# Whole rows normalised and stored beside the eighth expert's products, its slots' rows normalised singly and written over

## What is computed

```
x = x + xattn(layernorm(x), ctx)
h = layernorm(x)                                  # [4096, 256]
gates, idx = top_k(softmax(h @ wg), 2)            # renormalised
# every expert takes at most C = 1280 of its tokens
y = silu(disp @ fc1_w.T + fc1_b) @ fc2_w + fc2_b  # for each expert, 256 -> 1024 -> 256
res = h + sum over the two experts of gate * y
out = x + (res - mean(res)) * rsqrt(var(res) + 1e-5) * gamma + beta
```

## Time and profile before

| | |
|---|---|
| median of 3 runs | 764.63 us (762.34 to 767.64) |
| the profiled execution | 763.03 us, its span 761.3 us |
| busy PE / DVE / ACT / POOL | 672.8 / 551.4 / 409.8 / 419.7 us |
| mean granted clock of TensorE, share of full speed | 0.94 |
| DMA | 64.81 MB, mean 85 GB/s |

### The profile page before, as it was taken

The page is one execution under the profiler, slowest core; times in us unless marked ns, Lnnn a source line. Parts: engine busy times, 40 slices in busy tenths (PEclk is TensorE's granted clock), DMA queues, the critical chain, the costliest instruction groups (busy, mean ns, idle before and its releaser), DMA issues.

```text
span 761.3 us, 15549 instructions
## 1 busy us (share of the span) xinstructions
PE 672.8 (88%) x5562; PEld 643.6 (85%) x5562; DVE 551.4 (72%) x1129; ACT 409.8 (54%) x956; POOL 419.7 (55%) x541
## 2 busy tenths in 40 slices
PE   4999999999999645999999999999999999999500
PEld 3799999999988534999999998999999999999500
DVE  6578888888888795766566689687696566855187
ACT  6355555555555583545445475555555455634185
POOL 5445665665663426254544668576585653631456
PEclk9699999999999956999999999999999999999855
DMA  9710111111101124244334346453555342322474
GB/s 295 208 37 31 43 37 35 43 35 37 43 30 43 42 76 140 72 98 100 55 93 106 57 106 123 110 111 59 113 114 113 74 78 47 59 33 24 71 261 152
DMA packets 61348, 64.81 MB, mean 85 GB/s; under 512 B 15057, under 2 KB 56529, under 8 KB 61137
## 3 DMA queue, kind: packets, MB, share of 16 engines
q1 hardware_dynamic: 45201, 42.35, 17.7%
q0 software_dynamic: 15360, 21.31, 17.3%
q10 hardware_dynamic: 704, 0.01, 0.0%
HBM read 39.22 MB, written 23.72 MB: 83 GB/s over the span
## 4 chain that ended last, share of the span: by engine, by line
PE 84%; DVE 8%; DMA 3%; issue 2%; POOL 1%; ACT 1%; POOLq 0%; SPq 0%; DVEq 0%; ACTq 0%
PE banks L918 19%; PE banks L920 19%; PE banks L919 18%; PE banks L1054 8%; PE banks L1040 6%; PE banks L1028 5%; PE banks L1181 2%; DMA sum_rows<-y_sb,slot_ids 2%; PE banks L1090 1%; PE banks L941 1%; PE banks L963 1%; DVE oh_lo L1495 1%; DVE oh_id L1491 1%; DMA res<-sum_rows 1%; DVE z L1734 1%
## 5 line engine op out<-in xcount | busy, mean ns | idle before, releaser
L633 POOL DMA_INDIRECT sum_rows<-y_sb,slot_ids x80 | 131.0, 1638 | 164.0 <-ACT y_sb L861 147.5
L871 ACT ACTIVATE hraw<-banks,b_now 128x256 f32<-128x256 f32 x320 | 132.2, 476 | 90.1 <-PE banks L920 89.9
L918 PE MATMUL banks<-xT_hi,w_hi 128*128 128x256 f32 x560 | 161.8, 289 | 1.7 <-ACT xT_hi L843 1.7
L920 PE MATMUL banks<-xT_hi,w_lo 128*128 128x256 f32 x560 | 158.8, 284 | 0.0
L919 PE MATMUL banks<-xT_lo,w_hi 128*128 128x256 f32 x560 | 158.5, 283 | 0.0
L918 PE MATMUL banks<-w_hi,h_hi 128*128 128x256 f32 x528 | 149.0, 282 | 2.4 <-issue 1.6
L919 PE MATMUL banks<-w_lo,h_hi 128*128 128x256 f32 x528 | 148.7, 282 | 0.0
L920 PE MATMUL banks<-w_hi,h_lo 128*128 128x256 f32 x528 | 148.6, 281 | 0.0
L1700 DVE TENSOR_TENSOR h_lo<-hraw,h_hi 128x512 fp32r<-128x512 f32 x160 | 113.4, 709 | 5.5
L1698 DVE CAST h_hi<-hraw 128x512 fp32r<-128x512 f32 x160 | 79.4, 496 | 44.9 <-ACT hraw L871 44.2
L918 PEld LDWEIGHTS banks<-xT_hi,w_hi 128*128 128x128 f32 x560 | 106.5, 190 | 2.1 <-issue 2.1
(11 more groups left out here) (218 smaller groups left out, 1392.9 us busy)
## 6 DMA issues: line engine op xcount, KB each, us to landing
w1raw<-in_w1T SPq DMA_DIRECT2D x8, 1024.0 KB, 6.9
w2raw<-in_w SPq DMA_DIRECT2D x8, 1024.0 KB, 6.8
xn_rows<-xn SPq DMA_DIRECT2D x32, 128.0 KB, 1.7
sum_rows<-xn SPq DMA_DIRECT2D x32, 128.0 KB, 1.8
out<-z SPq DMA_DIRECT2D x16, 256.0 KB, 2.2
res<-sum_rows SPq DMA_DIRECT2D x7, 512.0 KB, 8.4
X<-in_x SPq DMA_DIRECT2D x2, 1280.0 KB, 12.5
xg<-xn_rows,slot_ids POOLq DMA_INDIRECT x80, 3.8
```

Source lines behind the costliest of these rows:

```text
L633: g.indirect_dma_start(sum_rows, bass.IndirectOffsetOnAxis(ap=slot_ids[:, st, 1, q:q + 1], axis=0), y_sb[:, u, q, :], None, bounds_check=N ...
L871: a.activation(hraw[:, j // 2, j % 2, :], banks[:, j // 2, (j % 2) * 256:(j % 2 + 1) * 256], ACT.Silu, bias=b1_now[:, (c // SPE) % 2, j:j ...
L918: t_.matmul(o, a_hi, b_hi, start=first, stop=False)
L920: return t_.matmul(o, a_lo, b_hi, start=False, stop=last)
```

## The change

The tail's work on whole rows moves to the steps of the eighth expert (supertiles 35 to 39), on sums which lack that expert. The eighth expert no longer scatters. Its slots' rows are gathered, completed, normalised one by one and written over the whole rows in the output.

- A new DRAM tensor `rest_rows` takes x + beta. SP stores four tiles of `X` to it in each expert's turn and the last four behind them.
- ScalarE makes the high part of h by a cast in steps 35 to 39 (`activation_hi`) in place of VectorE, and scales the results of supertile 34 at the start of step 36 instead of behind its SiLUs.
- When the scatters of supertiles 0 to 34 have landed, SP loads the 32 tiles (`wave`) into `w1raw`, `w2raw` and a new `late_rows`, which lies where the even experts' weights were; from tile 8 on only when the first four gathers of sums have landed. It stores the output in eight DMAs of four tiles.
- GpSimd gathers ten tiles of `sum_rows` by the slots of the eighth expert (`gather_sums`), four of them before the first power and six behind the second. For each quad it then makes a power two quads ahead, three products with gamma (`first_scaled`, was two), and for the first five quads gathers two tiles of `rest_rows` (`gather_rest`).
- VectorE works on quads in `wave_step`: two are begun at the end of each of steps 36 to 39 (statistics of two tiles in one instruction), their normalisation's bias and the one tile that it does alone follow a step later, their additions two steps later. ScalarE normalises three tiles of each quad at the end of steps 37 to 40.
- In place of bias, gate and scatter of the eighth expert VectorE adds gate * product to the gathered sums (`patch_sum`), and the bias b2 enters by one more product of TensorE with a row of ones, ten in all (K = 1, plain float32).
- Behind the last product VectorE normalises the ten patched tiles (`patch_begun`, `patch_done`), and GpSimd, once all stores of whole rows have landed, writes them over by ten indirect DMAs without addition (`scatter_patch`).

```diff
@@ block.sync
                 sp.dma_start(w2raw[:], w2[ds(e, 1)].rearrange("a (j p) d -> p (a j) d", p=P)).then_inc(load_w2, 16)
-
-            sp.wait_ge(scattered[0], 32 * (NST // 2))
-            sp.wait_ge(scattered[1], 32 * (NST // 2))
+                sp.wait_ge(sem("beta_added"), QT * e)
+                sp.dma_start(rest_t[:, ds(QT * (e - 1), QT), :], X[:, ds(QT * (e - 1), QT), 0:D]).then_inc(rests_stored, 16)
...
+            for u in range(2):
+                sp.wait_ge(scattered[u], 32 * ((SL + 1 - u) // 2))
...
             for n, (a, b) in enumerate(RES_LOADS):
-                sp.dma_start(res[:, a:b, :], sum_t[:, a:b, :]).then_inc(load_res[n], 16)
...
+                if a == 2 * QT:
+                    sp.wait_ge(sums_gathered[0], 16 * 2 * EARLY_SUMS)
+                sp.dma_start(wave(a, b), sum_t[:, a:b, :]).then_inc(load_res[n], 16)
+            for k in range(NQ):
+                sp.wait_ge(sem("out_made"), k + 1)
+                sp.dma_start(out_t[:, QT * k:QT * (k + 1), :], wave(QT * k, QT * (k + 1))).then_inc(stored, 16)
@@ block.gpsimd
+            for u in range(2):
+                pool.wait_ge(scattered[u], 32 * ((SL + 1 - u) // 2))
+            for m in range(EARLY_SUMS):
+                gather_sums(m)
+            deviations(0)
+            deviations(1)
+            for m in range(EARLY_SUMS, SPE):
+                gather_sums(m)
+            for k in range(NQ):
+                deviations(k + 2)
+                first_scaled(k)
+                if k < SPE:
+                    gather_rest(k)
+            patch_deviations(0)
+            patch_deviations(1)
+            pool.wait_ge(stored, 16 * NQ)
+            for m in range(SPE):
+                scatter_patch(m)
+                patch_deviations(m + 2)
@@ block.scalar
             def expert_step(gq, c):
                 rows_hi(gq, c + 1)
+                if c == SL + 1:
+                    scale_results(c - 2)
...
+                        if st >= SL and j % 2 and j > 1:
+                            activation_hi(st, j // 2 - 1)
+                    if st >= SL:
+                        activation_hi(st, HJ // 2 - 1)
...
+                k = 2 * (c - SL - 2)
+                if 0 <= k < NQ:
+                    first_normalised(k)
+                    first_normalised(k + 1)
@@ block.tensor
                     if used:
+                        if e == LAST:
+                            pe.wait_ge(load_b2, 16)
+                            pe.wait_ge(sem("zero_made"), 3)
+                            t_.matmul(o, ones_row[:], b2_sb[0:1, e, :], start=True, stop=False)
@@ block.vector
+            def wave_step(k):
+
+                if 2 <= k <= NQ:
+                    for n in (k - 2, k - 1):
+                        first_bias(n)
+                        last_done(n)
+                if 4 <= k <= NQ:
+                    first_done(k - 4)
+                    first_done(k - 3)
+                if k < NQ:
+                    quad_begun(k)
+                    quad_begun(k + 1)
...
+                elif within_st(gq, c - 2):
+                    patch_sum(c - 2)
                 rows_lo(gq, c + 1)
...
+                k = 2 * (c - SL - 1)
+                if 0 <= k <= NQ:
+                    wave_step(k)
...
+            patch_begun(0)
+            patch_begun(1)
+            first_done(NQ - 2)
+            first_done(NQ - 1)
+            for m in range(SPE):
+                if m + 2 < SPE:
+                    patch_begun(m + 2)
+                patch_done(m)
```

308 lines of the change are left out of this document (190 added, 118 removed).

## The result

| | before | after |
|---|---|---|
| median (lowest to highest) | 764.63 us (762.34 to 767.64, 7 runs) | 772.41 us (769.49 to 774.87, 7 runs) |
| ratio, 95% interval | | 1.0099 (1.007 to 1.0129) |
| span of the profiled execution | 761.3 us | 773.1 us |
| second scatter of supertile 33 starts | 665.71 | 670.22 |
| from there to the end of the span | 95.6 (forecast 92.1) | 102.9 |

What follows compares the result with a forecast made beforehand. GpSimd's list was taken as the new bound; with the tail behind it (758.9) and 0.5 for added stores the span summed to 759.4 against 761.3, 1.9 less, so 762.7, near 762.5; range 752 to 773 for 8 in 10.

Steps and rivals of the forecast that it cites:

- last scatter-add landed: From the second scatter of supertile 33 until supertile 34's last scatter-add has landed, at 674.3: 7.5 us.
- GpSimd's list: GpSimd's gathers, powers and gamma products beside the eighth expert, from 674.3 to 731.5: 57.2 us, the new bound.
- last product to last addition: From GpSimd's last gamma product (731.5) to VectorE's last addition (734.0), with patch work between: 2.5 us.
- to the first write: Last store of whole rows lands in 2.8 (736.8), then GpSimd starts writing patched rows at 737.6: 3.6 us.
- nine distances with powers: Ten indirect writes in a row, 1.62 apart (14.6), plus three powers between them (2.2): 16.8 us.
- last start to the end: Last indirect write's landing, 3.4, plus 1.1 to the end of the program: 4.5 us.
- Rival 2: Port contention slows GpSimd's gamma products; decides from 1.2 us each, time 774.5 at 1.3 each; chance 0.17.
- a hold of every product: Each of GpSimd's 24 gamma products waits for a full VectorE instruction of 0.70: time about 777.
- Bias products: Ten plain float32 products on TensorE at about 0.24 each, 2.4 us together, ending at 717.1 if left alone.
- The two stops: TensorE waits for patch sums in the eighth expert: 2.8 us for the first, some 5 for its last supertile.
- Rival 1: GpSimd keeps pace and TensorE stays the bound, products ending at 717.1: gain of 13.7, time 751; chance 0.17.
- rival 3: Added stores delay scatters and loads beside the experts: 9.3 us more than taken, time 772; chance 0.08.

Runs made afterwards that it cites:

- e1: Changed kernel without GpSimd's ten gathers of residual rows and the wait for them (incomplete result): 767.32 us, ratio to before 1.0048.
- e2: Changed kernel with GpSimd's 24 products with gamma on one column in place of 256 (incomplete result): 765.79 us, ratio to before 1.0013.
- e14: Changed kernel with only five of the ten patched row tiles written (incomplete result): 765.4 us, ratio to before 1.0019.
- e17: Changed kernel, complete, with several changes: gamma products shared with VectorE, split-format bias, additions ahead of most patches, earlier statistics and patch powers: 759.9 us, ratio to before 0.996.
- e16: Changed kernel, complete, with VectorE's additions of quads 6 and 7 moved ahead of the last patch sum and first two patches: 768.28 us, ratio to before 1.0073.
- e11: Changed kernel with GpSimd's 24 products with gamma replaced by constants written to scratch, reading nothing from SBUF: 767.76 us, ratio to before 1.0047.
- e5: Changed kernel, output complete, with all products with gamma of the whole rows moved from GpSimd to VectorE: 767.8 us, ratio to before 1.0056.
- e3: Changed kernel with all ten gathers of residual rows behind GpSimd's last product with gamma, nothing left out: 772.28 us, ratio to before 1.0111.
- e6: Changed kernel without TensorE's ten bias products (bias b2 of the eighth expert missing): 772.5 us, ratio to before 1.0117.
- e7: Changed kernel without the ten bias products and with products with gamma on one column only (incomplete result): 762.15 us, ratio to before 0.9978.
- e4: Kernel before with only the eight stores of residual rows to DRAM and their waits added: 764.92 us, ratio to before 1.0011.
- e9: Changed kernel, complete: gamma products on VectorE, bias as two split-format products, last additions and early patches ahead of the last patch sum: 764.76 us, ratio to before 1.001.

## Why the prediction was wrong

The path was the forecast one: GpSimd's list, then VectorE's last additions, the store, ten writes. It is e1, e2 and e14 that show it. Of 7.1 and 9.8 us taken from the list in the traces 5.1 and 6.6 came back, until TensorE was the next bound, and of five writes all. Two steps failed by their sizes. The one that decided it is the step from GpSimd's last product to VectorE's last addition, 2.5 in the sum and 6.7 in the trace: the prediction priced the contention on GpSimd's products alone, and it was VectorE that was held. The other is the list, 57.2 in the sum and 62.2 in the trace. Counted from the scatter of supertile 33, the sum gave 92.1 (758.9 - 666.8); the trace has 102.9. Another 3.4 of the trace lie ahead of that scatter (670.22 in place of 666.8), 2.2 before the experts and 1.2 within their unchanged steps; e17 has 0.2 of them.

| step | forecast | measured | difference |
|---|---|---|---|
| last scatter-add landed | 7.5 | 7.9 | +0.4 |
| GpSimd's list | 57.2 | 62.2 | +5.0 |
| last product to last addition | 2.5 | 6.7 | +4.2 |
| to the first write | 3.6 | 4.4 | +0.8 |
| nine distances with powers | 16.8 | 14.8 | -2.0 |
| last start to the end | 4.5 | 6.8 | +2.3 |

- **The list.** "Even if it waits for nobody" was its best case, and I took it for the likely one. The powers waited 2.6 for variances, and 5 of the gathers took 1.3 to 3.07 as recorded in place of about 1.05 (the longest stands in the timeline above). Some 2.3 of the 5.0 are this execution's: the same list ended 2.2 and 2.5 earlier in e14 and e16. Products at 0.80 and powers at 1.2 were right. The residual gathers took 13.0 to 13.9 in all between products that read, 11.1 between the constants of e11, and 10.4 in e5, where GpSimd makes no products; whether the reads stretched them is not shown.
- **VectorE's additions.** This is the step that decided it. Rival 2 put the price of the contention on GpSimd's products (1.2 each to decide); they stayed at 0.80. The loser was VectorE: from the last power to the last patch sum it took 7.8 (733.31 to 741.15) for six instructions which take 2.5 in e2 (727.84 to 730.35). e11 gives the price of the reads, some 4 us in all, 2.0 of them behind the last product; there this step still took 4.7, as VectorE then met TensorE's late end. The row that warned was on record: VectorE's product at 0.472 to 0.942. I read its maximum as rare. In the tail before GpSimd made two products at a time, and four only at the end; here it made nine in a row, though e1 and e3 show that such a row need not hold VectorE for 3.46. The prediction's figure for a hold of every product is also mis-added: 762.5 + 24 x 0.70 is 779, not 777.
- **The order.** I had seen that patch work stands ahead of the last additions and priced it, but did not ask what it costs once VectorE is late. e16 gives some 2 us back with one move.
- **The end.** 4.5 was a landing of 3.4 and the 1.1 that passed behind the last plain store (the rows give 1.3: 761.3 - 757.8 - 2.2). The last indirect write landed 2.4 behind its start, and the program ended 4.4 after that. From the start of the last write it is 6.8 to 6.9 in every run with ten writes but e1 (6.0). Why the end takes longer is open.
- **The writes.** 1.62 was taken between a gather and a scatter-add; they stand 1.28 to 1.59 apart where no power comes between, nearer to the gather. The time to the first write was short by 0.8, and that is the last store: issued at 747.1, it took 3.6 to land in place of 2.8, and the write started 0.8 later. Its row names VectorE's L1851 as releaser (6.14), but that pair had ended at 749.5, 2.0 ahead; in e16, where it was the last to come, the write followed 0.5 behind it.
- **Bias products.** Taken at 0.24 for each, 2.4 in all. The timeline of TensorE of after, around one pair of records, says otherwise:

```profile
707.23 0.28 PE L1004 MATMUL banks<-w_hi,h_lo 128*128 128x256 f32 x1
707.44 0.69 PE L1326 MATMUL banks<-b_sb,ones_row 1*128 1x256 f32 x2
708.06 0.39 PE L1002 MATMUL banks<-w_hi,h_hi 128*128 128x256 f32 x1
708.28 0.28 PE L1003 MATMUL banks<-w_lo,h_hi 128*128 128x256 f32 x1
```

  The next product starts 0.83 behind the one ahead of the pair in place of 0.12, and the one after it 0.22 later in place of 0.12, so each costs 0.8, some 8 in all. That, the half clock behind both stops, which the prediction did not price, and the later start put TensorE's end at about 739 (its busy time from 735 to 750 is 4.4) in place of 725. The two stops themselves were forecast (2.8 and some 5; 2.3 and 5.5 came). It cost nothing, as forecast (e6), but made TensorE the next bound once the list was shorter (e1, e2, e7). Rival 1's 751 was out of reach for that reason.
- **Right:** the casts on ScalarE (1.1), the free stores (e4, rival 3), the products' price, the patch chain behind TensorE's end (9.15 in rival 1, 9.9 to 10.0 measured).

The range (752 to 773) held 772.41 by 0.6, since it reached towards the contention case; that is luck more than insight, as the forecast of 762.5 was 9.9 too low. Of the signs named in the prediction, GpSimd's busy list, its waits, its products at 0.8 and the price of the writes came; TensorE ended 14 later, and the first load started at 678.55 instead of near 674, mostly by the later start.

## What to carry to other kernels

When work moves beside other work, write the list of the engine that gets it with its inputs' arrival times, not as a sum of durations; a sum is its lower bound. Price contention for both engines: here the one whose instructions kept their length held up the other. Look for the place where the one makes many products in sequence while the other has the path. Behind the last product of such a list every instruction counts: put what releases the last store first. And before a difference of two traces is explained, see where each profiled execution stands among its runs; here 2 us of the list were the single execution.

## What the runs showed of the hardware

- A VectorE instruction on 4 columns with two inputs in SBUF lasted 3.46 us beside GpSimd products of 0.79 each in a row, over four of them, and the following ones 0.96 to 1.23 in place of 0.42 to 0.68. In e14, e16 and e6 it was 3.46, 3.43 and 3.44; in e1 and e3 it was 0.68, and the nine products took 0.85 to 0.86 each. Beside constants written by GpSimd for 0.84 each it took 0.16. The Trainium skill (the section named above) has the second to come wait for the whole of the first; here the wait went over several instructions of GpSimd.
- Beside constants written by GpSimd a VectorE instruction with one tensor input (TENSOR_SCALAR, 128x4) took 2.08 and 2.10 in e11, to the end of the third constant in a row, where it takes 0.17 elsewhere. So writes alone can hold VectorE too.
- An indirect write without addition costs GpSimd 0.97 to 1.29, like a gather, against 1.55 to 1.84 for one with addition beside the eighth expert; from the start of the last one to the end of the program 6.8 us pass.
- One plain float32 product with a single row between others in the split format costs 0.7 to 0.8, though seven in sequence took 0.26 each. Two products of the split format with a single row (e9) cost hardly less: the next product starts 0.64 behind the one ahead of them, against 0.83.
- After stops of 2.3 and 5.5 us TensorE was granted 1.2 GHz in place of 2.4 (0.50 to 0.52) for some 7 and 5 us. After stops of 1.87 (e1) and 1.97 (e16) the clock stayed at 1.00.
